# Decoder layer, last batch: second weights issued behind each key store, zeros of spare rows issued behind the keys

## What is computed

```
x = layernorm(x + self_attention(x))                 # causal, 16 heads of 16, rotary
x = layernorm(x + cross_attention(x, ctx_2048))      # k, v = ctx @ wkv.T + bkv, 1500 rows a sequence
x = layernorm(x + experts(x))                        # 8 experts, the best 2 for each token:
                                                     # gelu(x @ w1 + b1) @ w2 + b2, F = 1024
```

## Time and profile before

| | us |
|---|---|
| median of three runs | 886.6 |
| lowest and highest run | 880.97, 889.96 |
| the profiled execution, its time | 884.88 |
| its span | 883.1 |
| TensorE busy in it | 800.3 |
| VectorE busy | 632.6 |
| ScalarE busy | 511.2 |

### The profile page before, as it was taken

One profiled execution on the slowest core, in us unless ns is written; L12 is line 12 of the kernel. 1 busy time (PEld: TensorE's weight loads), 2 busy tenths in 40 slices (PEclk: granted clock), 3 DMA queues, 4 the chain that ended last, 5 costly groups with the idle time before them and its releaser, 6 DMA issues.

```text
span 883.1 us, 30182 instructions
## 1 busy us (share of the span) xinstructions
PE 800.3 (91%) x12379; PEld 608.1 (69%) x12379; DVE 632.6 (72%) x1234; ACT 511.2 (58%) x1084; POOL 260.6 (30%) x334
## 2 busy tenths in 40 slices
PE   5689998999999989999899999999997789999996
PEld 3356766666666666666676666767665569999995
DVE  5866776768777767776777778776864736588887
ACT  2336655666566546655665665656664443687782
POOL 4233223222612251225123421522240103133332
PEclk9999999999999999999999999999999789999999
DMA  7355544554555554554555555545466855766653
GB/s 220 108 149 160 159 137 133 152 164 131 160 148 147 160 149 128 163 152 143 148 151 156 153 158 158 172 136 160 138 190 177 294 195 182 215 202 184 205 155 95
DMA packets 91377, 143.25 MB, mean 162 GB/s; under 512 B 11423, under 2 KB 79583, under 8 KB 87918
## 3 DMA queue, kind: packets, MB, share of 16 engines
q1 hardware_dynamic: 87742, 136.74, 51.8%
q0 software_dynamic: 3504, 4.62, 2.7%
HBM read 101.60 MB, written 39.68 MB: 160 GB/s over the span
## 4 chain that ended last, share of the span: by engine, by line
PE 40%; DMA 29%; DVE 10%; SPq 7%; ACT 7%; issue 5%; DVEq 0%; POOLq 0%; POOL 0%; ACTq 0%
DMA k_dram<-k_two 15%; DMA sums<-y_sb,g_token 9%; PE ps L1613 8%; PE ps L1606 7%; PE ps L1687 5%; SPq L1079 5%; PE ps L1665 4%; DMA k_st<-k_dram 4%; ACT k_two L1368 3%; DVE k_two L507 3%; PE ps L1629 3%; PE ps L1923 3%; DVE negmax L513 2%; PE ps L1944 2%; PE ps L1697 2%
## 5 line engine op out<-in xcount | busy, mean ns | idle before, releaser
L513 DVE TENSOR_REDUCE negmax<-ps 112x1 f32<-112x1500 f32 x121 | 207.3, 1713 | 44.4 <-PE ps L1629 44.1
L1395 ACT ACTIVATE pT<-ps 125x448 f32<-125x448 f32 x384 | 195.8, 546 | 18.6 <-PE ps L1665 14.7
L1230 POOL TENSOR_TENSOR ctx_lo<-ctx_raw,ctx_hi 128x250 f16<-128x250 f32 x188 | 119.3, 666 | 229.7 <-DVE ctx_hi L498 212.8
L1665 PE MATMUL ps<-qbd,k_st 97*128 97x112 f16 x1536 | 129.4, 216 | 20.2 <-ACT qbd L1351 10.8
L1665 PEld LDWEIGHTS ps<-qbd,k_st 97*128 97x128 f16 x1536 | 92.9, 99 | 78.0 <-ACT qbd L1351 27.1
L507 DVE SCALAR_TENSOR_TENSOR k_two<-ps,bk_sb,k_two 128x500 f16<-128x500 f32 x96 | 70.7, 736 | 96.7 <-ACT k_two L1368 96.7
L1368 ACT ACTIVATE k_two<-ps,bk_sb 128x500 f16<-128x500 f32 x96 | 65.1, 678 | 91.6 <-PE ps L1606 68.6
L1351 ACT COPY v_sb<-ps 125x512 f32<-125x512 f32 x96 | 56.3, 587 | 89.5 <-PE ps L1613 89.4
L1687 PE MATMUL ps<-pT,v_sb 125*17 125x56 f32 x6144 | 93.4, 217 | 10.1 <-issue 10.1
L1687 PEld LDWEIGHTS ps<-pT,v_sb 125*17 125x17 f32 x6144 | 81.5, 100 | 29.5 <-issue 19.2
L1629 PE MATMUL ps<-k_st,qbd 96*112 96x500 f16 x363 | 97.4, 375 | 3.7 <-DMA k_st<-k_dram 2.9
(11 more groups left out here) (258 smaller groups left out, 1396.0 us busy)
## 6 DMA issues: line engine op xcount, KB each, us to landing
k_st<-k_dram SPq DMA_DIRECT2D x288, 125.0 KB, 2.6
w_sb<-w SPq DMA_DIRECT2D x25, 1024.0 KB, 5.1
ctx_raw<-ctx_T SPq DMA_DIRECT2D x48, 500.0 KB, 4.5
k_dram<-k_two SPq DMA_DIRECT2D x96, 250.0 KB, 3.6
xs<-zeros SPq DMA_DIRECT2D x28, 260.0 KB, 3.1
w_sb<-w SPq DMA_DIRECT2D x8, 512.0 KB, 4.9
xg<-xs SPq DMA_DIRECT2D x21, 130.0 KB, 4.1
a_x<-x_tok SPq DMA_DIRECT2D x8, 128.0 KB, 2.8
```

What stands on the lines that cost most here:

```text
L513: V.tensor_reduce(negmax[0:QW], ps[0:QW, BANK_S:BANK_S + CHUNKS, 0:MC], AX.XY, ALU.max, negate=True).then_inc(max_done, 1)
L1230: last = nc.gpsimd.tensor_tensor(ctx_lo[:, k, c2, a], ctx_raw[:, k, c2, a], ctx_hi[:, k, c2, a], ALU.subtract)
L1395: nc.scalar.activation(pT[0:MT, (PAIRS * b + p) % 3, TPC * g:TPC * g + TPC], ps[0:MT, BANK_T + n % 2, 0:TPC * QW].rearrange("p (t n) -> p ...
L1665: last = mm(ps[:, BANK_T + n % 2, QW * i:QW * i + QW], k_st[:, j, p, a:a + P], qbd[:, j, p].rearrange("p h s -> p (h s)"), start=True, sto ...
```

## The change

In the last batch, `keys` takes a list of transfers and issues them behind the key store, ahead of SyncE's wait for it and of the three loads. The halves of the second weights, which were issued behind the loads, are given in this list; their number for each unit stays. The zeros of the spare rows and of the spare tile of sums, which were issued ahead of the first key unit, are issued behind the whole second weights. All other engines' programs stay.

```diff
-            def keys(b, par, u):
+            def keys(b, par, u, between=()):
 
                 c, g = UNIT[u]
                 i = key_place(par, c, g)
                 sp.wait_ge(unit_out, UNITS * b + u + 1)
                 sp.dma_start(k_dram[i], k_two[:, i]).then_inc(k_out[g], 16)
+                for dst, src in between:
+                    sp.dma_start(dst, src).then_inc(w2_ahead, 16)
                 sp.wait_ge(k_out[g], 16 * (CHUNKS * b + c + 1))
...
             two_batches(TILES - 2, last=True)
-            sp.dma_start(xs_tiles[E * REGION:].rearrange("g p n -> p g n"),
-                         zeros[:].unsqueeze(1).to_broadcast([P, XT - E * REGION, XW])).then_inc(spare_zeroed, 16)
-            sp.dma_start(sums_tiles[TILES], zeros[:, 0:D]).then_inc(sums_set, 16)
             half = FT // 2
             ahead = [(e, f) for e in range(E // 2) for f in (0, half)]
             sp.wait_ge(a_qlo_done, 2 * TILES)
             sp.wait_ge(a_x1_kept, TILES)
             for u, pieces in zip(KEY_UNITS, W2_AHEAD):
-                keys(B - 1, 1, u)
-                for e, f in ahead[:pieces]:
-                    sp.dma_start(w2_sb[:, e, f:f + half], w2[e, :, f:f + half]).then_inc(w2_ahead, 16)
+                keys(B - 1, 1, u, [(w2_sb[:, e, f:f + half], w2[e, :, f:f + half]) for e, f in ahead[:pieces]])
                 ahead = ahead[pieces:]
 
             sp.wait_ge(unit_done, UNITS * B)
             sp.wait_ge(ctx_lo_done, CHUNKS * B)
             for e in range(E // 2, E):
                 sp.dma_start(w2_sb[:, e], w2[e]).then_inc(w2_in, 16)
+            sp.dma_start(xs_tiles[E * REGION:].rearrange("g p n -> p g n"),
+                         zeros[:].unsqueeze(1).to_broadcast([P, XT - E * REGION, XW])).then_inc(spare_zeroed, 16)
+            sp.dma_start(sums_tiles[TILES], zeros[:, 0:D]).then_inc(sums_set, 16)
             keep_x2(TILES - 2, TILES - 1)
```

## The result

The changed kernel takes 875.71 us (median of 20 runs, 869.54 to 886.22), the kernel before 884.96 beside it (20 runs, 877.02 to 892.21). The ratio is 0.9905, with a 95% interval of 0.9877 to 0.9933: 8.4 us less (5.9 to 10.9), against 4.1 forecast. The profiled execution took 874.81 us (span 873.0). The ratios are those on record and not quotients of the medians, from which they differ by up to 0.3%.

What follows compares the result with a forecast made beforehand. It took the last batch's chain through key store, load, ScalarE's key step and qbd copy as the bound; 3.0 us of wait plus 1.1 of clock made 4.1, so 880.8 profiled, 882.5 for the median, range 877.0 to 888.5.

Steps and rivals of the forecast that it cites:

- The queue: SyncE's key rounds, last batch: unit 0's store lands 5.1 us earlier, unit 8's is issued at 671.0, its loads land about 679.4.
- The key wait gone, 3.0 us: ScalarE before unit 11's key step: the 3.33 us wait for unit 8's loads goes, so the qbd copy starts 3.0 us earlier.
- The clock, 1.1 us: TensorE behind the 3.33 us hole: without it the 96 value matmuls take 1.38 us instead of 2.44, giving 1.1 us.
- The other hole goes too: Rival, chance 0.25: TensorE's 3.01 us hole up to 677.03 goes as well, its code coming earlier; 7.7 us gained, 878.9.
- TensorE's code is held up longer: Rival, chance 0.12: the queue, full from 671 to 679, delays TensorE's code packet to 679.4; 888.3 us.
- The zeros: Moved behind the whole second weights: 4.2 us longer queue there, xg(0) still hidden with 1.3 us left.
- Unit 11's loads, "2 us left": Loads behind one half land near 691, before pair 4's scores need them at 693.3: hidden, 2 us left.

Runs made afterwards that it cites:

- b1: The kernel before, unaltered, run once more for a second trace; 893.91 us.
- e0: The changed kernel, unaltered, run again on another chip; 873.79 us against 886.33 for the kernel before, ratio 0.9855.
- e8: The changed kernel, unaltered, run a third time; 878.4 us against 883.5 for the kernel before, ratio 0.9953.
- e4: The changed kernel with four halves at unit 8 and none at units 6 and 11; 888.4 us against 887.3 for the kernel before, ratio 1.0012.
- e3: The kernel before with all eight halves behind unit 11's loads and the zeros moved as in the change; 885.89 us against 886.33, ratio 0.9964.
- e1: The kernel before with only the zeros moved, the halves staying behind the key loads; 884.07 us against 886.33, ratio 0.9965.
- b2: The kernel before with unit 5's half moved behind unit 11's loads; one time, 889.12 us, against a median of 887.3.
- e6: The kernel before with 50 small matmuls added in TensorE's hole during the key wait; 883.5 us against 883.5, ratio 1.002.
- e5: The changed kernel with no halves at units 8 and 11, their three shifted to the front; 882.1 us against 887.3 for the kernel before, ratio 0.9908.

## Why the prediction was wrong

The direction, the place and the cause were right; the size was half of what came, and the time fell below the range. Of the two terms of the sum the wait came out at its size, and the clock behind it was too small; the two as measured, 3.1 and 2.0, still don't add up to the 8.4 of the timed runs, whose interval begins at 5.9 (the two repeats of the changed kernel gave 12.9 and 4.2). In the traces the mean of before and b1 against the mean of after, e0 and e8 is 52.0 to 45.3 from A to D, 6.7 us: 5.2 from A to B, 2.0 from B to C, and 0.5 lost from C to D. Of the 5.2 the key wait is 3.1; the rest is the hole without a releaser with the clock behind it, 3.01 us long in one trace of before, which the change isn't shown to shorten. Step by step:

- **The queue.** Unit 0's store was to land by 648.5: 647.5, but this execution ran 1.5 us ahead, so by the clock of before that is 649.0; it took 3.6 us to land and not 2.6. Unit 8's was to be issued at 671.0; it was at 669.54, and with the same 1.5 us that is 671.0. Its loads were to land 8.4 us after that; the first is issued at 672.61, the last by 673.9, and the slowest took 4.5, so they are there near 678, 8.4 us after the store's issue. The steps of unit 8, on which the sum rests, held.
- **The key wait gone, 3.0 us**: the mechanism held, e4 shows it to be the cause, and the size held too. Four kernels with the same hole of 1.12 us tell it: from A to B e3, without the wait, takes 10.26 us, and e4, e1 and b2, with waits of 2.91, 3.27 and 3.51, take 12.95, 13.32 and 13.55, which is 2.7, 3.1 and 3.3 more, each time the wait less the 0.21 us that ScalarE still waits for the unit. b1 is 4.1 longer than the changed kernels (14.66 to 10.5 or 10.6), of which 3.2 are the wait, 0.3 the longer hole and 0.44 a hole of its own. In the timed runs the gain without the clock is 4.3 +-1.1 (e8) and 6.6 +-1.9 (e0); what may lie between that and 3.1 is not located.
- **The clock, 1.1 us: the step that failed.** The term was mis-sized, 1.1 us where the traces show 2.0, and the method was wrong with it. I counted one group of 96 matmuls at the place of the hole and took the clock to be as before from there on. But from B to C the kernel is not at one level for one group: 13.7 of 29.9 us before were low. Over the twelve traces without the xg wait, B to C is fixed by the low time, whichever kernel it is: 26.5 and 26.8 us at 3.4, 28.6 and 28.7 at 10.2, 29.6 to 29.9 at 13.7, 30.5 and 31.0 at 17.1, 30.9 to 31.1 at 20.0 to 20.5. That is 0.25 us for each us of low time. The six traces with a key wait had 17.6 us of it on average (13.7 to 20.5), the six without it 9.7 (3.4 to 17.1): 2.0 us, not 1.1. The timed runs point the same way: the mean clock is 0.9786 to 0.9826 where TensorE waits near a microsecond or more for a transfer there (e3, which waits for xg, among them) and 0.9836 to 0.9875 where it doesn't (over every run on record the two groups just meet, 0.9826 for e1 and 0.9820 for e8); the changed kernel is 0.0061 (e0) and 0.0024 (e8) above the kernel before beside it, worth 3.2 and 1.3 us. So in these two comparisons a quarter to a third of the gain is clock, and the clock is part of why they differ. This is a difference between groups and not a mechanism: with the hole filled (e6) the low time was the same 13.7 us, so that idling at this place brings the low level is not shown.
- **"The other hole goes too"** came nearest in size (7.7 us) and would have been read as confirmed from the first pair of traces: the hole fell from 3.01 to 1.40 and the low clock behind it went. That the packet of the instruction queue goes with the hole is borne out in all 13 traces; that the order of the halves makes it late is not. The hole is 1.67 in a second trace of the kernel before and 1.12 in e1, which has the old order of halves. I, too, had taken the 3.01 of one trace for a property of the kernel.
- **"TensorE's code is held up longer"**: no. With the queue full from 669.5 on the hole is 1.3 to 1.4, and the packet passes at 671.59 in 0.88 us, while unit 8's store and two halves are in flight. The Trainium skill, in the section "Queues, rings and completion order" of "DMA: Bandwidth & Descriptors", says that an engine takes turns between the rows that have work; this packet agrees with it.
- **The zeros.** I gave them no gain of their own at the front, which e1 bears out, and a cover of 1.3 us at the end. xg(0) is issued at 699.71, lands 3.7 us later at 703.41, and is taken at 705.34, with no wait: held, with 1.9 us left. Their price in the queue was over-estimated (4.2): the row sums right behind them land 3.5 us after the last whole weight, against 0.4 before, so 3.1. The base was off by more: the whole weights go out 9.1 us earlier than before (684.03, 693.17; 1.5 of it is this execution's own lead) and not 4.1, and xg(0) lands 7.3 earlier. SyncE is held 5.78 us in issuing the last of the zeros, which nobody waits for here.
- **Unit 11's loads, "2 us left"**: wrong. They landed 6.7 us after the first was issued and pair 4 waited 0.25 to 0.44 in three of the four traces of this order of halves (e8 is the one without). I had counted the half ahead of them and not the 4 MB queued right behind. It takes both: single loads took up to 5.8 us here, 2.8 to 3.6 behind one half with no bulk behind (unit 5), and 2.4 to 3.3 with the same 4 MB behind and no half ahead (e5).
- **The range.** Its low end came from a rival that asked for two mechanisms at once, less 2 for scatter. The clock of the whole stretch doesn't repair it: 13.7 us of low time at 0.25, 3.4 in place of 1.1, gives 880.2, and less 2 that is 878.2, still above 875.7. Of the distance 1.6 us are the base: the forecast started from a median of three, 886.6, and the 20 runs beside the changed kernel have 885.0; the ratio, taken of 886.6, gives 878.2, inside the range.

What stays open: the 3 us between the two terms as measured and the 8.4 of the first timed runs, and what makes the low level come. It is less where the key wait is gone, on average, but one kernel had 3.4 and 17.1 us of it in two traces, and filling the hole (e6) didn't help. The profiles also start the last batch anywhere from 638.8 to 652.6 us, before anything of the change acts, and I can't say what of the 0.9855 on one chip and the 0.9953 on another comes from there.

## What to carry to other kernels

When one queue issues a store, waits for it and then loads it back, put bulk transfers behind the store and ahead of the loads, as many as the slack of the load hides: SyncE stands through the store's landing, so what is ahead of the store delays the whole round, and what is behind it uses the time in which SyncE would stand. Look for the next cover that goes: 2 MB ahead of the loads brought the whole wait back, 8 MB at the end made a new one of 7 us. Before pricing a gap of one trace, take a second trace of the same kernel: one hole here was 3.0 and 1.7 us. Beside every wait that goes, look at the clock over the whole stretch behind it and not over the first group, and take what it may give back as a range: one kernel had 3.4 and 17.1 us of low time in two traces.

## What the runs showed of the hardware

- A 250 KB key store to DRAM lands in 2.2 to 3.1 us with no halves between the keys (e3), in 2.5 to 3.8 (once 4.4, e0) with one or two halves of 0.52 MB behind each store (after, e0, e8), and in 4.4 to 6.6 at units 2 to 8 where halves are issued right ahead of it (before, b1, b2, e1, e6). Three 125 KB loads take 2.2 to 3.8 with no half ahead, 2.8 to 5.9 behind two halves, 6.6 to 6.9 behind four.
- TensorE had a hole of 1.1 to 2.0 us (once 3.0) at the same matmul of its program in all 13 traces, with no semaphore to wait for; it ended 1.2 to 1.6 us after a 16 KB packet of the instruction queue. With 50 matmuls added to the program another one, 0.44 us in one trace and absent from the rest, was 1.94.
- The mean granted clock of a run goes with its time: 0.01 less is 5.2 to 5.6 us more of 880. In a stretch where TensorE trades work with two other engines the 1.2 GHz level costs only 0.25 us for each us of it (26.46 and 30.52 us at 3.4 and 17.1); VectorE is busy 20.0 us in it at either level.
